# An attention block on one core: the convolution's rectifiers one step later, and a tail with three bank pairs in which TensorE and ScalarE finish GpSimd's pieces

## The reference

```
out = bilinear_resize(x, 64, 64)
out = relu(bn1(conv1x1(out, conv1_w)))
q, k, v = 1x1 convolutions of out (32, 32 and 256 channels), N = 64 * 64 = 4096 positions
attn = softmax(q^T k); out = gamma * (v attn^T) + out
out = relu(bn2(out))
out = bn3(conv1x1(out, conv2_w))
return relu(bilinear_resize(out, 128, 128) + x)
```

## Time and profile before

| what | value |
| --- | --- |
| median of 3 runs | 2357.51 us |
| the profiled execution's own time | 2359.95 us |
| its span | 2358.1 us |
| TensorE busy | 2288.7 us, 97% |
| VectorE busy | 1778.8 us, 75% |
| ScalarE busy | 1713.8 us, 73% |
| GpSimd busy | 1687.3 us, 72% |

### The profile page before, as it was taken

The page is one execution under the profiler, slowest core; times in us unless marked ns, Lnnn a source line. Parts: engine busy times, 40 slices in busy tenths (PEclk is TensorE's granted clock), DMA queues, the critical chain, the costliest instruction groups (busy, mean ns, idle before and its releaser), DMA issues.

```text
span 2358.1 us, 48231 instructions
## 1 busy us (share of the span) xinstructions
PE 2288.7 (97%) x15970; PEld 1648.5 (70%) x15970; DVE 1778.8 (75%) x3286; ACT 1713.8 (73%) x3313; POOL 1687.3 (72%) x1610
## 2 busy tenths in 40 slices
PE   4889999999999999999999999999999999999998
PEld 2467777777567777777747777777765777777774
DVE  7676588887568888888657888888756777777778
ACT  5577777777657777777756777777765777777773
POOL 7994478888379988888628988888845444444464
PEclk9999999999999999999999999999999999999999
DMA  6312122323103322332202322322310121222322
GB/s 210 111 54 64 36 68 102 107 98 108 36 30 109 109 102 101 107 107 96 101 1 72 109 96 101 107 98 107 107 54 1 65 71 63 71 72 71 143 90 108
DMA packets 59273, 204.11 MB, mean 87 GB/s; under 512 B 8752, under 2 KB 9840, under 8 KB 59120
## 3 DMA queue, kind: packets, MB, share of 16 engines
q1 hardware_dynamic: 41696, 138.93, 18.2%
q10 hardware_dynamic: 17424, 63.45, 6.6%
HBM read 135.24 MB, written 67.11 MB: 86 GB/s over the span
## 4 chain that ended last, share of the span: by engine, by line
PE 87%; DVE 5%; ACT 3%; POOL 2%; issue 1%; SPq 1%; DMA 1%; DVEq 0%; ACTq 0%; POOLq 0%
PE acc L1184 19%; PE acc L1186 19%; PE acc L1185 18%; PE et L1053 10%; PE emx L1041 6%; PE wrk L1075 5%; PE acc L1103 3%; PE wrk L1041 3%; PE acc L1095 2%; PE wrk L1066 1%; PE acc L1087 1%; DVE qs L795 1%; DVE ks L795 1%; ACT qs L542 1%; ACT qs L541 1%
## 5 line engine op out<-in xcount | busy, mean ns | idle before, releaser
L1184 PE MATMUL acc<-vh,ph 128*128 128x257 f16 x4096 | 1120.0, 273 | 1.3 <-DVE vl L812 1.1
L1186 PE MATMUL acc<-vh,pl 128*128 128x257 f16 x4096 | 1116.1, 272 | 0.0
L1185 PE MATMUL acc<-vl,ph 128*128 128x256 f16 x4096 | 1110.8, 271 | 0.0
L470 ACT ACTIVATE ph<-et 128x512 f16<-128x512 f32 x1024 | 610.8, 596 | 297.6 <-PE et L1053 288.6
L754 DVE TENSOR_TENSOR pl<-et,ph 128x512 f16<-128x512 f32 x1024 | 701.9, 686 | 146.6 <-ACT et L471 144.2
L471 ACT ACTIVATE et<-et 128x512 f32<-128x512 f32 x1024 | 606.9, 593 | 0.0
L1185 PEld LDWEIGHTS acc<-vl,ph 128*128 128x128 f16 x4096 | 400.9, 98 | 277.5 <-issue 20.5
L1184 PEld LDWEIGHTS acc<-vh,ph 128*128 128x128 f16 x4096 | 400.2, 98 | 70.0 <-issue 11.0
L1186 PEld LDWEIGHTS acc<-vh,pl 128*128 128x128 f16 x4096 | 395.4, 97 | 56.3
L382 POOL TENSOR_TENSOR ct<-cd,uw 128x512 f32<-128x512 f32 x246 | 325.3, 1344 | 125.3 <-DVE xres L785 119.7
L1053 PE MATMUL et<-qs,ks 98*128 (+1 forms) x1024 | 390.0, 381 | 4.1 <-DVE pl L754 3.5
(11 more groups left out here) (145 smaller groups left out, 2677.7 us busy)
## 6 DMA issues: line engine op xcount, KB each, us to landing
xres<-in_x SPq DMA_DIRECT2D x139, 512.0 KB, 4.5
out<-xres ACTq DMA_DIRECT2D x121, 512.0 KB, 2.6
xin<-in_x SPq DMA_DIRECT2D x110, 512.0 KB, 3.7
xr<-in_x SPq DMA_DIRECT2D x7, 512.0 KB, 7.3
out<-xr SPq DMA_DIRECT2D x6, 512.0 KB, 2.6
out<-xr SPq DMA_DIRECT2D x2, 256.0 KB, 2.1
osb<-in_L_conv_conv_w SPq DMA_DIRECT2D x1, 256.0 KB, 7.6
osb<-in_L_conv_v_w SPq DMA_DIRECT2D x1, 256.0 KB, 7.7
```

The lines of the kernel that those rows point to most:

```text
L470: ops.activation(ph[:, t % 4, :], et[t % 2][:, :], ACT.Exp)
L1184: mm(acc[it][:, 0:C + 1], ph[:, tt % 4, pt], vh[:, tt, 0:C + 1], start=tt == 0, stop=False)
L1185: mm(acc[it][:, 0:C], ph[:, tt % 4, pt], vl[:, tt, :], start=False, stop=False)
L1186: last = mm(acc[it][:, 0:C + 1], pl[:, tt % 4, pt], vh[:, tt, 0:C + 1], start=False, stop=tt == JT - 1)
```

## The change

It has two parts.

In the blocks, `relu_h` comes at steps `T_RELU` = (4, 8) instead of 3 and 7. This holds for all 28 blocks with c > 0, two rectifiers each.

In the tail:
- `late_bank` goes through three pairs of banks, (acc0, acc1), (acc2, acc3), (wrk, emx), instead of two. The first use of (wrk, emx) waits for bn3; after that a shortcut waits until the piece three back was read out.
- VectorE makes the two residuals before its four additions of piece 120 instead of between them.
- The second `LATE_V` piece's weighting moves from VectorE to ScalarE (`late_weights(1)`), and VectorE takes that piece's differences ahead of the first piece's columns.
- For GpSimd's two pieces TensorE adds the column products too (`late_products`, one more pair of identity matmuls each), and ScalarE reads the banks with a ReLU into `late_x` (`late_rectified`), counted by the new semaphore `late_out`. VectorE's `late_sums` handles only its own five.
- TensorE's order in the tail is written out: the shortcut of the next piece stands ahead of the interpolation of the current one.

The diff:

```
--- before.py
+++ after.py
@@ -133,6 +133,7 @@
         ot_rdy, ot_done, h_rdy = sem("ot_rdy"), sem("ot_done"), sem("h_rdy")
         cv_rdy, y_rdy = sem("cv_rdy"), sem("y_rdy")
         late_ld, late_zero, late_xy, late_stored = sem("late_ld"), sem("late_zero"), sem("late_xy"), sem("late_stored")
+        late_out = sem("late_out")
         late_d, late_w, late_y, late_c, late_p = (sem(n) for n in ("late_d", "late_w", "late_y", "late_c", "late_p"))
 
         def at_least(eng, s, value):
@@ -204,7 +205,15 @@
         late_cd = et[1][:, 0:UR * (S - 1)].rearrange("p (r c) -> p r c", c=S - 1)
 
         def late_bank(i, part):
-            return acc[i % 2 * 2 + part]
+            return ((acc[0], acc[1]), (acc[2], acc[3]), (wrk, emx))[i % 3][part]
+
+        def late_written(eng, i, parts=2):
+
+            done = LATE_ORDER[:i]
+            if LATE_ORDER[i] in LATE_V:
+                eng.wait_ge(up_added, LATE * 2 + 2 * sum(u in LATE_V for u in done) + parts)
+            else:
+                eng.wait_ge(late_out, 2 * sum(u in LATE_POOL for u in done) + parts)
 
         def kept(ck):
 
@@ -323,11 +332,11 @@
             for i, u in enumerate(LATE_ORDER):
                 _, half, _, row = late_place(u)
                 if u != LATE_ORDER[-1]:
-                    sp.wait_ge(up_added, (LATE + i + 1) * 2)
+                    late_written(sp, i)
                     sp.dma_start(dram_rows(out, B - 1, half, row, UR), late_x[:, i]).then_inc(late_stored, 16)
                     continue
                 for part in range(2):
-                    sp.wait_ge(up_added, (LATE + i) * 2 + part + 1)
+                    late_written(sp, i, part + 1)
                     sp.dma_start(dram_rows(out, B - 1, half, row + part * (UR // 2), UR // 2),
                                  late_x[:, i, part * (UR // 2):(part + 1) * (UR // 2), :]).then_inc(late_stored, 16)
             for s in range(4):
@@ -596,8 +605,8 @@
                 t_cv, t_store = T_CV_LAST if is_last(b, c) else T_CV, store_steps(g)
                 before = [before[j] for j in before if j >= len(store_steps(g - 1))]
                 for t in range(JT):
-                    if c > 0 and t in (T_OT[0] + 2, T_OT[1] + 2):
-                        relu_h(g - 1, T_OT.index(t - 2))
+                    if c > 0 and t in T_RELU:
+                        relu_h(g - 1, T_RELU.index(t))
                     if t in (t_cv[0] + 1, t_cv[1] + 1) and not (isinstance(g, int) and g == 0):
                         bn3(g - 1, (c - 1) % 2, t_cv.index(t - 1), c == 1, c == 0)
                     if t in t_store and t_store.index(t) in ups:
@@ -631,7 +640,9 @@
             bn3(NB * B - 1, (NB - 1) % 2, 0, False, True)
             bn3(NB * B - 1, (NB - 1) % 2, 1, False, True)
             store(0, LATE - 1, B - 1, (LATE - 1) // PIECES % NB, (LATE - 1) % PIECES)
-            for d in range(ROWS_BY_V, len(LATE_V)):
+
+            def late_weights(d):
+
                 _, _, first, _ = late_place(LATE_V[d])
                 act.wait_ge(late_d, d + 1)
                 act.wait_ge(late_y, d)
@@ -639,6 +650,22 @@
                     for parity, weight in enumerate((-(first + r) / (H - 1), (S - 1 - first - r) / (H - 1))):
                         last = ops.activation(late_rt[:, r, parity, :], late_rd[:, d % 2, r + parity, :], ACT.Copy, scale=weight)
                 last.then_inc(late_w, 1)
+
+            def late_rectified(u):
+
+                i = LATE_ORDER.index(u)
+                act.wait_ge(late_xy, i + 1)
+                for part in range(2):
+                    rs = slice(part * (UR // 2), (part + 1) * (UR // 2))
+                    ops.activation(late_x[:, i, rs, :].rearrange("p r c -> p (r c)"), late_bank(i, part)[:, :],
+                                   ACT.Relu).then_inc(late_out, 1)
+
+            late_weights(1)
+            late_weights(2)
+            late_weights(3)
+            late_rectified(LATE_POOL[0])
+            late_weights(4)
+            late_rectified(LATE_POOL[1])
 
         @block.vector
         def _(dve):
@@ -942,31 +969,24 @@
 
                 i = LATE_ORDER.index(u)
                 dve.wait_ge(late_xy, i + 1)
-                if u in LATE_V:
-                    d = LATE_V.index(u)
-                    dve.wait_ge(late_p, d + 1)
-                    products = late_ct[:, d % 2]
-                else:
-                    dve.wait_ge(up_p, (LATE + LATE_POOL.index(u) + 1) * UP)
-                    products = ct[:, u % 2]
+                d = LATE_V.index(u)
+                dve.wait_ge(late_p, d + 1)
+                products = late_ct[:, d % 2]
                 for part in range(2):
                     rs = slice(part * (UR // 2), (part + 1) * (UR // 2))
                     ops._custom_dve(bass.dve_ops.TENSOR_ADD_SAT, out=late_x[:, i, rs, :].rearrange("p r c -> p (r c)"),
                                     in0=late_bank(i, part)[:, :], in1=products[:, rs].rearrange("p r c two -> p (r c two)"),
                                     s0=HUGE, s1=0.0).then_inc(up_added, 1)
 
-            add_piece(0, LATE - 1, 0)
-            add_piece(0, LATE - 1, 1)
             residual(NB * B - 1, NB - 1, 0)
             residual(NB * B - 1, NB - 1, 1)
-            add_piece(0, LATE - 1, 2)
-            add_piece(0, LATE - 1, 3)
+            for part in range(4):
+                add_piece(0, LATE - 1, part)
             late_differences(0)
             late_weighted(0)
             late_rows(0)
+            late_differences(1)
             late_columns(0)
-            late_differences(1)
-            late_weighted(1)
             late_rows(1)
             late_sums(LATE_V[0])
             late_differences(2)
@@ -975,13 +995,11 @@
             late_rows(2)
             late_differences(3)
             late_columns(2)
-            late_sums(LATE_POOL[0])
             late_sums(LATE_V[2])
             late_rows(3)
             late_differences(4)
             late_columns(3)
             late_sums(LATE_V[3])
-            late_sums(LATE_POOL[1])
             late_rows(4)
             late_columns(4)
             late_sums(LATE_V[4])
@@ -1228,7 +1246,10 @@
 
             def late_shortcut(i):
 
-                at_least(pe, up_added, (LATE + i - 1) * 2 if i > 1 else 0)
+                if i == 2:
+                    pe.wait_ge(y_rdy, 2 * NB * B)
+                elif i > 2:
+                    late_written(pe, i - 3)
                 for part in range(2):
                     mm(late_bank(i, part)[:, :], ident[:, :],
                        late_x[:, i, part * (UR // 2):(part + 1) * (UR // 2), :].rearrange("p r c -> p (r c)"), start=True, stop=False)
@@ -1236,7 +1257,8 @@
             def late_interpolated(i):
 
                 u = LATE_ORDER[i]
-                if u in LATE_V:
+                own = u in LATE_V
+                if own:
                     pe.wait_ge(late_y, LATE_V.index(u) + 1)
                     rows = late_y2[:, LATE_V.index(u) % 2]
                 else:
@@ -1245,16 +1267,38 @@
                 for part in range(2):
                     twice = rows[:, part * (UR // 2):(part + 1) * (UR // 2), :].unsqueeze(3).broadcast_to([P, UR // 2, S, 2])
                     last = mm(late_bank(i, part)[:, :].rearrange("p (r c two) -> p r c two", c=S, two=2), ident[:, :], twice,
+                              start=False, stop=own)
+                if own:
+                    last.then_inc(late_xy, 1)
+
+            def late_products(i):
+
+                u = LATE_ORDER[i]
+                pe.wait_ge(up_p, (LATE + LATE_POOL.index(u) + 1) * UP)
+                for part in range(2):
+                    last = mm(late_bank(i, part)[:, :], ident[:, :],
+                              ct[:, u % 2, part * (UR // 2):(part + 1) * (UR // 2)].rearrange("p r c two -> p (r c two)"),
                               start=False, stop=True)
                 last.then_inc(late_xy, 1)
 
             late_shortcut(0)
             for half in range(2):
                 conv2(NB * B - 1, half)
+            late_shortcut(1)
             late_interpolated(0)
-            for i in range(1, len(LATE_ORDER)):
-                late_shortcut(i)
-                late_interpolated(i)
+            late_shortcut(2)
+            late_interpolated(1)
+            late_shortcut(3)
+            late_interpolated(2)
+            late_products(2)
+            late_interpolated(3)
+            late_shortcut(4)
+            late_interpolated(4)
+            late_shortcut(5)
+            late_interpolated(5)
+            late_shortcut(6)
+            late_products(5)
+            late_interpolated(6)
 
 
 FIRST_LOADS = (0, 3, 1, 2, 6, 4)
@@ -1329,6 +1373,7 @@
 
 AHEAD = 3
 T_OT = (1, 5)
+T_RELU = (4, 8)
 T_CV = (20, 22)
 
 
@@ -1384,7 +1429,6 @@
 LATE = pieces_until(NB * B - 1) + 1
 LATE_V = tuple(LATE + i for i in (0, 3, 5, 4, 6))
 LATE_POOL = tuple(LATE + i for i in (1, 2))
-ROWS_BY_V = 2
 LATE_ORDER = (LATE_V[0], LATE_V[1], LATE_POOL[0], LATE_V[2], LATE_V[3], LATE_POOL[1], LATE_V[4])
```

54 lines of the change are left out of this document (30 added, 24 removed).

## The result

The changed kernel took 2345.6 us (median of 4 runs, 2344.01 to 2346.84), where the forecast was 2344.8; the kernel before took 2359.47 beside it (4 runs, 2357.0 to 2361.59). These medians lie 13.9 apart. The ratio measured is 0.9947, with a 95% interval from 0.9934 to 0.9959: faster by some 12.5 us, and by 9.7 to 15.6 within the interval. The profiled execution of the changed kernel took 2346.84 us with a span of 2344.8, that of the kernel before 2359.95 with 2358.1: 13.1 less in time and 13.4 in span, where the sum said 12.7.

The account below looks back on a forecast made before the run. TensorE, busy 97% of the span, was taken as the bound: 6.0 + 5.1 in the blocks and 1.6 in the tail make 12.7, so 2344.8 us from the median 2357.51; range 2342.5 to 2354.5.

Parts of the forecast that it names:

- the sum: Whole kernel: 6.0 and 5.1 us gained in the blocks plus 1.6 in the tail, 12.7 in all.
- The first wait: Fourth score unit in 24 blocks, late behind ScalarE's copy and rectifier: 0.25 us each goes, 6.0 in all.
- The second wait: TensorE's gaps before the energies of steps 9 and 10 in 16 blocks: 0.32 us each goes, 5.1 in all.
- Rival A: Blocks: only the 0.25 us waits go, VectorE stays as late against TensorE; 7.6 us gained, 2349.9; chance 0.22.
- rival B: Step 7 meeting: GpSimd's L345 gets in first, 16 blocks pay back the 0.25; 3.6 us gained, 2353.9; chance 0.13.
- The margin of 0.12: Step 7 in the blocks: VectorE's addition L782 would ask 0.12 us before GpSimd's L345.
- The second rectifier at step 8: ScalarE in the blocks: moving it from step 7 leaves the same work ahead of step 9, so it costs nothing.
- Rival C: Blocks: rectifier at step 8 delays the copy the two-unit steps need, by 0.72 in 24 blocks; 2367.2; chance 0.06.
- D: Blocks: the change does nothing there, the 0.25 has another cause; 1.6 us gained, 2355.9; chance 0.05.
- The tail: After the last block: convolution earlier, TensorE becomes the bound, last sum at 2352.65 instead of 2354.25; 1.6 us gained.
- The alternative in which TensorE does not bind the tail: Tail, by the skill page's 216 ns matmul: last sum is VectorE's own, 3.9 us earlier, whole gain 14.9.

Follow-up runs that it names:

- Two maxima: Changed kernel with two maxima over 128 columns on VectorE ahead of step 7's addition, in blocks with score units: 2354.01 against 2357.78 us, ratio 0.9983.
- two bank pairs: Changed kernel with two bank pairs in the tail instead of three: last sum 36.4 us after the first transpose (a single execution).
- four memsets: Changed kernel with four one-column memsets on VectorE ahead of step 7's addition, in blocks with score units: 2347.23 against 2361.16 us.
- the first rectifier alone: Kernel before with the first rectifier moved to step 4, the second still at 7, old tail: 2345.88 against 2357.32 us, ratio 0.9953.
- the blocks' part alone: Kernel before with the rectifiers at steps 4 and 8, tail as before: 2346.62 against 2357.32 us, ratio 0.9954.
- additions first: Changed kernel with two additions of piece 120 ahead of the residuals again: last sum 35.2 us after the first transpose (a single execution).

## Why the prediction was right

- **The first wait, 24 x 0.25 = 6.0.** It held: the copy left the rectifier's shadow, all 24 units are at a pitch of 0.11. The eight blocks that had only this wait went from 61.25 to 61.0.
- **The second wait, 16 x 0.32 = 5.1.** It held, and by the steps that were given: GpSimd's time pinned (825.01 for 1.49, as the earlier trace rows had 829.40 for 1.23 with the start 0.25 later), VectorE asking 0.12 ahead (0.14 in fact), an addition of 0.73, the low part at 831.88 (836.0 less the 4.14 by which this block started earlier is 831.9). The next addition did not take 1.6 but 1.27, since GpSimd's instructions had moved too. Rival A wanted another meeting that costs TensorE time, rival B a lost race; there was neither. The row on which the forecast rested B's rejection is read a little wrong: at 874.66 GpSimd's L377 is recorded 5 ns ahead of VectorE's L785, not behind it, and VectorE was served first all the same, so that row supports the step more than the text says. Two maxima ahead of the addition, with which VectorE loses the race, bring the waits back in these 16 blocks alone. B was close, though: the lead was 0.06 in two blocks of the changed kernel and 0.01 in the first block of the third batch (1335.61) with two bank pairs, and with four memsets one block lost the race. The margin of 0.12 was worked out for one block, and that the two with half of it went the same way is in part luck.
- **The second rectifier at step 8: nothing.** Right: it costs nothing and gives nothing, and the forecast had laid the gain wholly on the first. Rival C, a copy delayed at step 9, is out, and so is D, by the first rectifier alone.
- **The tail, 1.6.** 1.5 by the profiles. The convolution starts 3.05 after the first transpose (3.06 by the text), the fourth rows are there after 22.65 (22.55), TensorE waits 0.51 (0.5), and from there to the last sum it is 10.6. The alternative in which TensorE does not bind the tail, put at 14.9 (its own terms, 11.1 + 3.9, give 15.0), is out: VectorE waits 4.17 for TensorE.
- **What the sum had not.** By the spans the gain is 13.4, 0.7 more than the sum. In the blocks it is 11.3 instead of 11.1, in the tail 1.5 instead of 1.6. The remaining 0.6 stands ahead of the first transpose (194.79 before, 194.16 now), in a part that the change does not touch; over the other kernels of this study that place lies between 192.99 and 195.14. It is scatter and not gain.
- **The absolute number.** 2344.8 was forecast and 2345.6 measured. That this is only 0.8 off is partly luck: the forecast took 12.7 from a median of 2357.51, and the kernel before, run beside the change, came to 2359.47, as its runs lie near 2357 and near 2361. The mechanism is confirmed by the blocks and the tail, not by this closeness.
- **A small slip.** The exponentials' distance in the earlier trace rows is 0.47, not the 0.49 of the text; the 1.7 us that it rounds to stands.

## What to carry to other kernels

A small wait of the bounding engine can stand for a larger loss two engines on: here 0.25 us of it fixed the moment at which VectorE and GpSimd met, and removing it gave 0.57 a block, the 0.25 included. Such a meeting can tip the other way by a few hundredths of a microsecond, so look at its margin in every block and not in one. So before pricing a shift, list which of the engines behind it are led by the bounding one and which are pinned by something else; the meetings between the two kinds are what changes. And when work is moved off an engine to relieve it, stop at the piece where the new engine becomes the bound: the first of the two pieces paid here, the second cost 1.7 us.

## What the runs showed of the hardware

- A VectorE addition with both inputs in SBUF and a GpSimd instruction take turns, and who comes first decides. Started 0.14 before GpSimd's, it takes 0.73 and GpSimd's 1.27 grows to 1.73; started 0.26 after, it takes 1.56, and started 0.03 after, 1.80. The 0.4 between 0.14 before and 0.26 after was worth 0.58 us a block at steps 9 and 10. Within a hundredth of a microsecond the recorded starts do not tell who goes first (the 5 ns of 874.66). The Trainium skill, SBUF — State Buffer (Who interferes with whom), states such a lock, held for the whole instruction by whichever issues first; the trace agrees (1.56 against 0.73).
- Memsets of one column are nearly free on VectorE when what follows does not depend on them: four moved the next start by 0.04 us. They are no delay to measure with; a maximum over 128 columns is (0.38 for two, 0.77 for four).
- TensorE's granted clock was not the same in all executions. In the profile of the kernel before it stood at the lower level (1.2 GHz) for 3.4 us from 1182.7 on, at the turn from the second to the third batch, right behind a gap of TensorE of 2.14 us; in the profile with the first rectifier alone it stood at 2.4 GHz there, behind a gap of 1.80. The same four matmuls behind the gap, in the kernel before and in that one:

```profile
1182.79 3.60 PE L1087 MATMUL acc<-xr,w1t 128*128 128x512 f32 x4 [2.14 <-issue]
```
```profile
1175.34 1.98 PE L1087 MATMUL acc<-xr,w1t 128*128 128x512 f32 x4 [1.80 <-issue]
```

  The profiles of the kernel before and of the changed one both have the lower level there, so it cancels between them. The stretch between the first transposes around it (1130.58 to 1186.22) is 55.64 us long in the profile of the kernel before and 53.68 in the other: 2 us, about the scatter between runs of one kernel.
- The old tail lets TensorE idle 2.1 us before the last convolution. In the profile of the blocks' part alone the clock was at the lower level for 3.4 us from 2313.4 on, and the first four matmuls took 2.84 in place of 1.98:

```profile
2312.45 2.84 PE L1075 MATMUL wrk<-hbuf,w2t 128*128 128x512 f32 x4 [2.10 <-ACT hbuf L483]
```

  Yet that tail was 0.9 shorter than the one of the kernel before, which had the full clock. The two profiles with one rectifier moved have the old tail and the lower level at this place too, and theirs are 0.0 and 0.2 shorter. From the first transpose to the last sum it is 33.95 us with the blocks' part alone, 34.80 and 34.61 in those two, and 34.81 in the kernel before. In all three VectorE starts its second piece later (L910, 9.34, 10.18 and 10.00 after the first transpose instead of 9.04), as bn3 is late. From there to the fourth rows (L927) it needs 14.37 us instead of 15.52, since it meets GpSimd elsewhere: the column differences, for one, take 1.51 and 1.10 where they took 1.78 and 1.76. From the fourth rows to the last sum it is 10.2 in all four. So a small delay of VectorE shortened the stretch, and a larger one gave back what was won. Of the ten profiles with the changed tail none has the lower level at the convolution, though in one of them (additions first) TensorE waits 2.11 there, and 0.24 in the others.
